# Cross attention of a decoder layer: the exponential reads the score banks, VectorE bounds its result in place

## The reference

```python
q = proj(x, Wq, bq); k = proj(ctx, Wk, bk); v = proj(ctx, Wv, bv)
scores = einsum('bhsd,bhtd->bhst', q, k) / sqrt(32)
scores = clip(scores, -50, 50)
scores = where(attend, scores, -10000.0)
scores = clip(scores, -50, 50)
probs = softmax(scores); probs = probs / (probs.sum(-1) + 1e-8)
delta = rs * (einsum('bhst,bhtd->bhsd', probs, v) @ Wo.T + bo)
x = layernorm(x + layernorm(delta) * ln_gamma + ln_beta)
```

## Time and profile before

| | |
|---|---|
| executions | 1523.41, 1525.0, 1523.33 us; median 1523.41 |
| profiled execution | 1524.37 us, span from first to last instruction 1522.5 |
| mean granted TensorE clock | 0.970 of full speed |
| busy | PE 1388.2, DVE 1231.4, ACT 801.8, POOL 741.3 us |
| cross attention in the span | from about 1000 to 1338 us |

### The profile page before, as it was taken

One profiled execution on the slowest core, in us unless ns is written; L12 is line 12 of the kernel. 1 busy time (PEld: TensorE's weight loads), 2 busy tenths in 40 slices (PEclk: granted clock), 3 DMA queues, 4 the chain that ended last, 5 costly groups with the idle time before them and its releaser, 6 DMA issues.

```text
span 1522.5 us, 24965 instructions
## 1 busy us (share of the span) xinstructions
PE 1388.2 (91%) x8338; PEld 1090.1 (72%) x8338; DVE 1231.4 (81%) x1990; ACT 801.8 (53%) x1798; POOL 741.3 (49%) x781
## 2 busy tenths in 40 slices
PE   5899999999999999999999999889999997459986
PEld 4788888888888888888888888767777775213332
DVE  6988888888888888888887888647788888669996
ACT  4444444545445444455555455445655555248884
POOL 4434335235334334333443433354677775547984
PEclk9999999999999999999999999989999999679998
DMA  5401101011011010021112011230000004014433
GB/s 209 164 3 42 56 15 42 28 42 42 28 42 41 29 42 15 15 70 56 36 45 101 14 62 35 76 112 15 15 15 14 14 1 173 0 26 96 88 86 94
DMA packets 73380, 79.92 MB, mean 52 GB/s; under 512 B 46006, under 2 KB 46518, under 8 KB 72892
## 3 DMA queue, kind: packets, MB, share of 16 engines
q1 hardware_dynamic: 73276, 78.73, 17.0%
HBM read 59.83 MB, written 8.40 MB: 45 GB/s over the span
## 4 chain that ended last, share of the span: by engine, by line
PE 45%; DVE 32%; issue 11%; POOL 7%; ACT 3%; DMA 1%; DVEq 1%; SPq 0%; POOLq 0%; ACTq 0%
PE psum L326 9%; PE psum L328 8%; PE psum L327 8%; DVE rope_b L513 6%; PE psum L942 3%; PE psum L367 3%; DVE p L522 3%; DVE total_e L526 3%; DVE acc L556 2%; PE psum L943 2%; PE psum L944 2%; DVE s L494 2%; PE psum L388 2%; DVE rope_a L513 2%; DVE xinv L1095 2%
## 5 line engine op out<-in xcount | busy, mean ns | idle before, releaser
L730 POOL TENSOR_TENSOR qk<-rope_a,rope_b 128x512 f32<-128x512 f32 x128 | 177.2, 1384 | 569.2 <-DVE rope_b L513 569.2
L326 PE MATMUL psum<-x_hi,w_hi 128*128 128x512 f32 x512 | 210.3, 411 | 11.2 <-POOL w_lo L724 11.2
L328 PE MATMUL psum<-x_hi,w_lo 128*128 128x512 f32 x512 | 201.6, 394 | 0.0
L327 PE MATMUL psum<-x_lo,w_hi 128*128 128x512 f32 x512 | 200.7, 392 | 0.0
L513 DVE SCALAR_TENSOR_TENSOR rope_b<-psum,qk_bias,sin 64x512 f32<-64x512 f32 x256 | 192.0, 750 | 3.7
L604 ACT ACTIVATE e<-s 128x384 f32<-128x384 f32 x128 | 66.3, 518 | 243.1 <-DVE s L494 243.1
L494 DVE SCALAR_TENSOR_TENSOR s<-psum,tri 128x384 f32<-128x384 f32 x128 | 70.7, 552 | 121.5 <-PE psum L367 121.5
L326 PE MATMUL psum<-w_hi,x_hi 128*128 128x256 f32 x512 | 147.4, 288 | 0.0
L327 PE MATMUL psum<-w_lo,x_hi 128*128 128x256 f32 x512 | 144.7, 283 | 0.0
L328 PE MATMUL psum<-w_hi,x_lo 128*128 128x256 f32 x512 | 144.6, 282 | 0.0
L618 ACT ACTIVATE e<-p 128x128 f32<-128x128 f32 x128 | 39.3, 307 | 184.5 <-DVE p L522 184.5
(11 more groups left out here) (184 smaller groups left out, 3883.7 us busy)
## 6 DMA issues: line engine op xcount, KB each, us to landing
stage<-w_self_dram SPq DMA_DIRECT2D x64, 256.0 KB, 2.9
w_raw<-w_ffn_dram SPq DMA_DIRECT2D x32, 512.0 KB, 3.7
acc<-xT_dram SPq DMA_DIRECT2D x4, 1024.0 KB, 7.7
acc<-x_dram SPq DMA_DIRECT2D x1, 4096.0 KB, 15.0
w_signs<-w_sign SPq DMA_DIRECT2D x16, 256.0 KB, 2.2
c_raw<-ctxT_dram SPq DMA_DIRECT2D x8, 512.0 KB, 3.6
xstage<-w_cross_dram SPq DMA_DIRECT2D x16, 256.0 KB, 3.0
w<-w_signs SPq DMA_DIRECT2D x2, 2048.0 KB, 11.8
```

Source lines behind the costliest of these rows:

```text
L326: pe.matmul(ps, ah, bh, start=n == 0, stop=False)
L327: pe.matmul(ps, ah, bl, start=False, stop=False)
L328: last = pe.matmul(ps, al, bh, start=False, stop=n == len(pairs) - 1)
L730: nc.gpsimd.tensor_tensor(qk[:, k % 2, which, :], rope_a[:, which, :], rope_b[:, which, :], ALU.add).then_inc(qk_ready, 1)
```

## The change

`exps` reads the score banks itself: it waits for `s_mm` and writes `e` in SBUF. `clip` now works in place on `e`, SBUF to SBUF, behind the exponential of its half, and bounds at exp(-50) and exp(50), which gives the same values since the exponential rises with its argument. The semaphore `clipped` becomes `exped` and is signalled by ScalarE; `e_ready`, for which `mix` and `sum_e` wait, is signalled by `clip`. `score` of the next chunk waits for the exponentials of this one. In VectorE's `emit` the clip is moved from the front of the step to behind `norm` (and behind `take_mask`, and `take_x` at i=2). One semaphore of `x1_norm` is merged into another, with other counts.

```diff
@@ tensor, score @@
-                wait(pe, clipped, (b * CH + c) * HALVES)
+                wait(pe, exped, (b * CH + c) * HALVES)
@@ vector @@
             def clip(b, c):
-                dve.wait_ge(s_mm, b * CH + c + 1)
-
                 for kt in range(HALVES):
-                    nc.vector.tensor_scalar(e[:, c % 2, :, kt * S:(kt + 1) * S], scored[:, :, kt, :], LIMIT, -LIMIT,
-                                            ALU.min, ALU.max).then_inc(clipped, 1)
+                    dve.wait_ge(exped, (b * CH + c) * HALVES + (kt + 1))
+                    part = e[:, c % 2, :, kt * S:(kt + 1) * S]
+                    nc.vector.tensor_scalar(part, part, EXP_MOST, EXP_LEAST, ALU.min, ALU.max).then_inc(e_ready, 1)
@@ vector, emit @@
                 for i in range(CH):
-                    if live(b):
-                        clip(b, i)
                     if i == 3 and live(b + 1):
                         take_mask(b + 1, 1 - par)
...
                     if i == 2 and live(b + 1):
                         take_x(b + 1, 0)
                         take_x(b + 1, 1)
+                    if live(b):
+                        clip(b, i)
@@ scalar, x1_norm @@
-                nc.scalar.activation(less[:, 0, :], rstd[:, 0, :], ACT.Identity, scale=-1.0).then_inc(less_ready, 1)
-                act.wait_ge(less_ready, b + 1)
+                nc.scalar.activation(less[:, 0, :], rstd[:, 0, :], ACT.Identity, scale=-1.0).then_inc(x1_shifted, 1)
+                act.wait_ge(x1_shifted, b * 3 + 1)
...
-                act.wait_ge(x1_shifted, b * 2 + 2)
+                act.wait_ge(x1_shifted, b * 3 + 3)
@@ scalar, exps @@
-                act.wait_ge(clipped, (b * CH + c) * HALVES + (kt + 1))
-                part = e[:, c % 2, :, kt * S:(kt + 1) * S]
-                nc.scalar.activation(part, part, ACT.Exp, scale=mask_now[:, par, kt, 0:1],
-                                     bias=mask_now[:, par, kt, 1:2]).then_inc(e_ready, 1)
+                if kt == 0:
+                    act.wait_ge(s_mm, b * CH + c + 1)
+                nc.scalar.activation(e[:, c % 2, :, kt * S:(kt + 1) * S], scored[:, :, kt, :], ACT.Exp,
+                                     scale=mask_now[:, par, kt, 0:1], bias=mask_now[:, par, kt, 1:2]
+                                     ).then_inc(exped, 1)
```

More of the change, by code:

```diff
@@ L1 @@
+import math
 from contextlib import ExitStack
@@ L789, in cross_attention @@
     LIMIT = 50.0
+    EXP_MOST, EXP_LEAST = math.exp(LIMIT), math.exp(-LIMIT)
     v_proj = env["shared_sems"]["v_proj"]
@@ L861, in cross_attention @@
         s_mm = sem("s_mm")
-        clipped = sem("clipped")
+        exped = sem("exped")
         e_ready = sem("xe_ready")
@@ L880, in cross_attention @@
         scaled = sem("scaled")
-        less_ready = sem("less_ready")
         x1_shifted = sem("x1_shifted")
```

## The result

Four executions of the changed kernel took 1534.68 to 1541.73 us, median 1539.4, beside a median of 1524.2 for the kernel before (four executions): ratio 1.0089, 95% interval 1.0076 to 1.0102. The change makes the kernel 0.9% slower. The forecast was 1535.3, in a range of 1525.5 to 1544.5. The profiled execution is the fastest of the four, 1534.68 with a span of 1532.9, 10.3 us more than the profiled execution of before.

The account below looks back on a forecast made before the run. TensorE, busy 35.0 of 37.1 us a period, and an almost closed ring through GpSimd, TensorE, VectorE and ScalarE bound the kernel. Full periods +8.8, head +1.4, tail +1.7 gave +11.9: 1535.3 us, range 1525.5 to 1544.5.

Parts of the forecast that it names:

- closed second ring: Cross attention, beside TensorE: `sum_e`, ones product, `norm`, clip, exponential, next `sum_e`, almost without slack; +2.2 us per period.
- GpSimd's loss: GpSimd operations held up by VectorE's in-place SBUF clip: an estimated 0.55 us lost per half clip.
- leg B: End of `sum_e`(b,0) to end of `sum_e`(b,1): 12.9 us against 12.04, +0.9, with TensorE waiting 0.8.
- A: End of `sum_e`(b,1) to start of `sum_e`(b,2): 5.7 us against 4.38, +1.3.
- C: Start of `sum_e`(b,2) to end of `sum_e`(b,3): 13.1 us against 11.91, +1.2, the clip waiting for `c_lo`.
- D: End of `sum_e`(b,3) to end of `sum_e`(b+1,0): 7.6 us against 8.77, −1.2, the exponential long done.
- half clock: Rival, chance 0.12: TensorE's clock falls after its waits around chunk 3; +0.9 us in four periods, 1538.9.
- Head: Batches 0 and 1: only chunk 3 of batch 1 meets `c_lo`; +1.4 us.
- tail: Batches 6 and 7, to the end of the last `norm`: together +1.7 us.
- PSUM rate: Rival, chance 0.08: the in-place clip takes 1.21 us and shares nothing with GpSimd; +3.7 per period, 1544.
- no meeting: Rival, chance 0.12: the clips fall in GpSimd's pauses and never meet it; +0.6 us in four periods, 1526.
- faster case: Rival, chance 0.08: TensorE alone is the bound; its waits of 1.07 and 0.54 go in five periods, 8 us, 1515.

Follow-up runs that it names:

- the waits filled: Changed kernel plus idle TensorE products ahead of the v part (8) and ones part (16) of chunk 3, batches 0 to 5: 1533.5 us, ratio 1.0062.
- the last experiment: Kernel before, with the new clip form and place for chunk 0 alone and `scale_y` moved behind both exponentials: 1518.7 us, ratio 0.9960.

## Why the prediction was right, and what in it was off

*The bound.* The closed second ring was the right reading. Between `sum_e`(2,0) and `sum_e`(6,0) the four periods add 9.6 us (8.8 forecast), ahead of that 1.2 (1.4).

*The clip.* 0.67 forecast. In after, the two lines that changed give (ns min/median/max):

```profile
L1089 DVE TENSOR_SCALAR xe<-xe x64: 679/687/2570, 1020.3 to 1314.6; 128x1024 f32<-128x1024 f32 x64
```

```profile
L1290 ACT ACTIVATE xe<-psum,mask_now x64: 1185/1202/1227, 1019.1 to 1310.4; 128x1024 f32<-128x1024 f32 x64
```

Median 0.687, longest 2.57; the exponential is 0.04 shorter than in the earlier trace rows, inside the bounds of 0.1.

*GpSimd's loss.* Forecast 0.55 per half clip and 0.9 for leg B; measured 0.33 (`y,beta`) and 0.45 (root), B +0.77. The term was a little too large, and I had read the earlier trace rows wrongly: I held the loss against the whole length of VectorE's operation, where what counts is what is left of it when GpSimd issues. There `y,gamma` is issued with 0.44 left of the first `x2_norm` (0.54 from 1327.00) and loses 0.29. The first clip ends at 1103.21, 0.48 after `y,beta` is issued; the second ends at 1106.45, 0.59 after the root is issued. Each time GpSimd loses all of what is left but 0.15. VectorE does no worse: a clip that stood behind GpSimd ends 0.56 after GpSimd is done, 0.13 less than its own 0.687. The Trainium skill (SBUF — State Buffer, Who interferes with whom) has the second to issue blocked until the first has finished, whichever engine it is. The trace agrees in both directions, up to these 0.13 to 0.15; I was wrong to say that it shows less on GpSimd's side. The loss is below 0.67 here because each clip has itself stood behind GpSimd first and is in its last 0.5 to 0.6 when the next operation of GpSimd is issued.

*Legs.* At the upper clock A 5.46 (5.7), B 12.79 (12.9), C 13.04 (13.1), D 7.26 (7.6). `c_lo` is what the clip of chunk 3 waits for: it ended 9.23 into the leg (9.4). `norm` ended at 7.7, not 8.7, and this error is hidden by the wait. The 0.8 us that TensorE was to wait in B did not come: TensorE works through B and is done about when the ring is. The sum of the four is 38.5 (39.3), so 5.7 us in four periods where I had 8.8.

*The signs named beforehand.* Periods are 38.5 to 40.2, the clip has durations from 0.68 to 2.57, `finish_y`'s operations are longer. One sign holds in part only: GpSimd is busy through the wait of 2.02, but in the wait of 1.19 only until 1124.03, the first 0.6; then it waits for the clips too.

*The step that failed* is the weight of the half clock. I made it a rival of 0.12, for all periods or none, working through leg B. It is there in both profiled executions of the changed kernel, in three and in four of the four periods, and works in leg D. Timeline of after, two legs D behind the same wait, first the one at half clock and then the one at the upper level:

```profile
1205.72 1.08 PE L1028 MATMUL psum<-e_sum,ones 128*32 128x256 f32 x8 [2.02 <-POOL e_sum L1358]
...
1208.39 0.41 PE L944 MATMUL psum<-c_lo,xw_hi 128*128 128x256 f32 x1
...
1209.70 0.47 ACT L1241 ACTIVATE kT<-psum,xk_bias 128x256 f32<-128x256 f32 x1 [4.50 <-PE psum L945]
...
1211.30 0.69 DVE L1089 TENSOR_SCALAR xe<-xe 128x1024 f32<-128x1024 f32 x1 [1.44 <-ACT xe L1290]
...
1212.08 2.39 POOL L1358 TENSOR_TENSOR e_sum<-xe 128x1024 f32<-128x1024 f32 x1 [5.54 <-DVE xe L1089]
```

```profile
1128.69 0.28 PE L944 MATMUL psum<-c_lo,xw_hi 128*128 128x256 f32 x1
...
1130.19 0.47 ACT L1241 ACTIVATE kT<-psum,xk_bias 128x256 f32<-128x256 f32 x1 [2.95 <-PE psum L945]
...
1130.56 1.20 ACT L1290 ACTIVATE xe<-psum,mask_now 128x1024 f32<-128x1024 f32 x1
...
1131.36 1.29 DVE L1089 TENSOR_SCALAR xe<-xe 128x1024 f32<-128x1024 f32 x2
```

At the lower level (1.2 GHz) a K product takes 0.41 (0.28 at 2.4 GHz) and the first K projection ends 4.0 us after `sum_e`, against 2.35. `take_k` stands ahead of the second exponential in ScalarE's queue, so exponential, clip and `sum_e` all move; at 2.4 GHz the second exponential ends at 1131.76, just before its half of the clip can start, and `norm` is what the clips wait for. My sentence that the exponential is "long done" in D was wrong: at the upper level it is 0.3 us ahead, at the lower one the clip waits 1.44 for it. D gives back 1.5 us there, and only 0 to 0.7 where the clock falls. The three slow legs D account for 3.5 us in the profiled execution. A slow D also leaves TensorE behind, which shows in leg A; in the fourth period it comes 0.5 us late to the ones product and A is 5.88 instead of 5.46:

```profile
1224.89 2.38 POOL L1358 TENSOR_TENSOR e_sum<-xe 128x1024 f32<-128x1024 f32 x1
...
1227.78 0.61 PE L1028 MATMUL psum<-e_sum,ones 128*32 128x256 f32 x8
```

With the waits filled D is 7.3 and A 5.45 every time, which shows the cause. That the clock loses some legs in one execution and others in the next would also give the spread of 7 us between executions; that is argued from the clocks listed with them (0.965 and 0.964 in the two of 1534.7 and 1537.1, 0.959 and 0.960 in the two of 1541.7).

*The ends.* Head +1.2 (+1.4), a hit by luck: the terms that the prediction names for it, +1.2 for leg C and half of D's 1.2 back, give 0.6 and not 1.4, and the trace has other parts, A +1.35 and +0.76 in batches 0 and 1, C −1.15 and +0.61. The tail, up to the last `norm`, came out at −0.9 instead of +1.7: B of batch 6 +1.0 (0.9), A +0.9 (1.3), C and D of batch 6 17.5 instead of 19.85 (18.2 forecast), B of batch 7 +0.9, the rest 19.2 instead of 20.49 (20.7 forecast). Behind the last `norm` come another +0.4. Why C and D of batch 6 and the rest behind batch 7's B are shorter than my chains was not tested. This error of 2.6 and the one on the legs, 3.1, outweigh the clock's 3.5, and so the profiled execution took 1534.7 where the sum said 1536.3. The median, 1539.4, is 4.7 higher. That the profiled execution had more of its legs at the upper clock than the others fits its mean clock, the highest of the four, but the others have no trace. The median stands nearest to the 1538.9 of the half-clock rival; its number is right by luck too, since its way, B bound by TensorE, is not what happened.

*Rivals.* The PSUM rate, no meeting and the faster case are refuted by the rows above. "TensorE's waits go, 8 us" did not come true in the changed kernel, and in part in the last experiment, by 6.

*Open:* why behind the same 2.02 us wait the clock falls in one period and not in the next. `take_x` first together with `scale_y` late wasn't run, nor the changed kernel with `c_lo` at another place.

## What to carry over

Before an operation is exchanged for a cheaper one, ask which engine shares what it uses now: an SBUF-to-SBUF `tensor_scalar` of 0.69 us made the legs in which GpSimd is never idle 0.8 and 0.4 us longer than one of 1.18 out of PSUM at the same place, and the other two legs shorter. Cut the period at the hand-offs of the second-busiest ring and price the legs; a wait that is removed (61 us of it here) buys only what the next in each queue lets through, and that was one step of four. New waits of TensorE of one or two microseconds belong in the sum twice, once as they are and once as the matmuls behind them at half clock, followed through the queue of the engine that drains them.

## What the runs showed of the hardware

- VectorE's in-place clip and GpSimd's operations wait for each other's end, less 0.13 to 0.15 us. VectorE: 2.74 for a pair of 1.28, behind `c_lo`. GpSimd: 0.33 and 0.45 us lost where 0.48 and 0.59 of a clip were left. Out of PSUM the pair runs beside `c_lo` in 2.34, and `c_lo` in 2.37.
- A wait of 2.02 us of TensorE is followed by the lower clock in some periods and not in others (0.41 and 0.28 us for the same product): in three of four periods of one execution and in all four of another.
- The exponential of 128x1024 out of PSUM takes 1.20, out of SBUF 1.24.
- Idle products in TensorE's waits bring every full period to 38.5 us, where most were 39.2 to 40.2 without them, and the median down by 4 us (1537.5 to 1533.5).
